# VectorE reads a chunk's second pair of value tiles out of the side bank ahead of rounding the first-layer keys' high part

## The reference, cut to what matters

```
x = x + L0_xattn(layernorm(x), ctx)     # rotary positions, a distance bias, softmax, gate
x = x + L0_ffn(layernorm(x))            # three products, tanh
x = x + L1_xattn(layernorm(x), ctx, ctx, mask)
x = x + L1_ffn(layernorm(x))            # 8 experts, the best 2 of each token

# L0_xattn, for each of 4 batches, 16 heads of 8
kv_in = layernorm(ctx, gamma, beta)
k = rope(kv_in @ Wqkv[D:2*D].T)
v = kv_in @ Wqkv[2*D:].T
attn = softmax(q @ k.T * SCALE + temporal_bias)
attended = attn @ v
```

## Time and profile before

| | |
|---|---|
| time, median of 3 runs | 558.69 us (555.54 to 559.5) |
| profiled execution, its own time | 558.84 us |
| its span, first to last instruction | 557.2 us |
| TensorE busy | 508.0 us, 91% |
| ScalarE busy | 434.7 us, 78% |
| VectorE busy | 280.2 us, 50% |
| GpSimd busy | 169.0 us, 30% |
| mean granted TensorE clock | 0.977 of 2.4 GHz |
| chain that ended last | PE 53%, ACT 12%, DVE 10%, issue 9%, POOL 8%, DMA 5% |

### The profile page before, as it was taken

How to read it: one execution, slowest core, us unless ns; L and a number is a source line. 1 busy time by engine, 2 the same in 40 slices (tenths; PEclk the granted TensorE clock), 3 DMA queues, 4 the chain that set the end, 5 groups by cost and what they waited for, 6 DMA issues and landing times.

```text
span 557.2 us, 15361 instructions
## 1 busy us (share of the span) xinstructions
PE 508.0 (91%) x6338; PEld 260.7 (47%) x6338; DVE 280.2 (50%) x739; ACT 434.7 (78%) x496; POOL 169.0 (30%) x202
## 2 busy tenths in 40 slices
PE   7788998999899898998999999899899989998995
PEld 4444545445445454554555444344443444443343
DVE  5858566874776356653522342336243533440354
ACT  1257486787678787888998999899989998999832
POOL 4468637584785308840110001000000000000000
PEclk9789899999899999999999999999999999999996
DMA  8579885389558314580745291249123910000000
GB/s 269 160 230 288 225 273 138 129 283 292 148 192 285 124 49 126 197 261 17 140 105 188 69 211 40 87 113 223 33 65 76 235 32 8 6 1 2 6 6 16
DMA packets 51584, 74.53 MB, mean 134 GB/s; under 512 B 11146, under 2 KB 40050, under 8 KB 51506
## 3 DMA queue, kind: packets, MB, share of 16 engines
q1 hardware_dynamic: 40258, 37.54, 26.9%
q0 software_dynamic: 5632, 24.07, 12.9%
q10 hardware_dynamic: 5616, 11.86, 7.0%
HBM read 39.95 MB, written 18.83 MB: 106 GB/s over the span
## 4 chain that ended last, share of the span: by engine, by line
PE 53%; ACT 12%; DVE 10%; issue 9%; POOL 8%; DMA 5%; ACTq 1%; SPq 1%; DVEq 0%; POOLq 0%
PE ps L539 24%; PE ps L515 16%; ACT probs L1171 7%; DVE k_swapped L1480 2%; DMA q_side<-in_far_q 2%; PE ps L669 2%; ACT ctx_turned L1171 2%; PE ps L440 2%; DMA ctx_tokens<-in_ctx_rows 2%; DVE row_stats L1442 1%; POOL k L1025 1%; PE ps L450 1%; ACT ctx_tokens L1171 1%; DVE k_parts L1497 1%; POOL k L1023 1%
## 5 line engine op out<-in xcount | busy, mean ns | idle before, releaser
L1171 ACT ACTIVATE probs<-ps 124x1024 f32<-124x1024 f32 (+1 forms) x305 | 295.7, 1024 | 54.2 <-PE ps L520 41.1
L515 PE MATMUL ps<-q_side,k_side 64*124 64x256 bf16 (+1 forms) x1664 | 159.9, 291 | 20.9 <-ACT probs L1171 12.1
L539 PE MATMUL ps<-probs,values 124*9 124x256 f32 (+1 forms) x2440 | 163.7, 383 | 0.0
L515 PEld LDWEIGHTS ps<-q_side,k_side 64*124 64x124 bf16 (+1 forms) x1664 | 80.0, 131 | 124.7 <-ACT probs L1171 62.0
L539 PEld LDWEIGHTS ps<-probs,values 124*9 124x9 f32 (+1 forms) x2440 | 52.9, 90 | 65.6 <-issue 15.5
L1054 POOL TENSOR_TENSOR post_rstd<-post_rstd,power 128x2 f32<-128x2 f32 x12 | 8.5, 712 | 194.0 <-DVE post_rstd L1695 126.5
L520 PE MATMUL ps<-bias_near,bias_w 64*124 64x84 bf16 (+1 forms) x416 | 42.5, 200 | 0.0
L1171 ACT ACTIVATE ctx_tokens<-ps 124x1024 f32<-124x1024 f32 (+1 forms) x37 | 37.9, 1026 | 4.9 <-PE ps L515 4.0
L1480 DVE SCALAR_TENSOR_TENSOR k_swapped<-ps,beta_products,k_table_sb 32x496 f32<-32x496 f32 (+2 forms) x64 | 40.4, 632 | 0.9
L1171 ACT ACTIVATE ctx_turned<-ps 124x1024 f32<-124x1024 f32 (+1 forms) x37 | 37.9, 1024 | 3.4 <-PE ps L515 2.4
L1171 ACT ACTIVATE ctx_normed<-ps 124x1024 f32<-124x1024 f32 (+1 forms) x37 | 37.9, 1025 | 2.4 <-PE ps L515 1.6
(11 more groups left out here) (256 smaller groups left out, 621.0 us busy)
## 6 DMA issues: line engine op xcount, KB each, us to landing
k_side<-k_scratch SPq DMA_DIRECT2D x24, 400.2 KB, 7.8
k_scratch<-k_parts POOLq DMA_DIRECT2D x16, 372.0 KB, 5.4
k_side<-k_parts SPq DMA_DIRECT2D x45, 124.0 KB, 2.5
q_side<-q_parts SPq DMA_DIRECT2D x63, 64.0 KB, 2.7
v_scratch<-values POOLq DMA_DIRECT2D x4, 936.0 KB, 10.9
values<-v_scratch SPq DMA_DIRECT2D x4, 936.0 KB, 14.4
v_scratch<-v POOLq DMA_DIRECT2D x12, 288.0 KB, 5.8
mask_q<-in_mask POOLq DMA_DIRECT2D x8, 400.5 KB, 4.4
```

Source lines behind the costliest of these rows:

```text
L515: last = pe.matmul(ps[0:width, bank, SQ * i:SQ * (i + 1)], kst[rows, j % 2, 2 * g + i, at], qst[rows, query_slot(j, run), 2 * g + i, :], s ...
L539: last = pe.matmul(ps[32 * i:32 * i + VC, ACC + g // 2, SQ * (g % 2):SQ * (g % 2) + SQ], v[0:rows, j % 2, t, h, :], probs_of(u)[0:rows, SQ ...
L1171: act.activation(probs_of(u)[0:rows, :], ps[0:rows, s:s + 2, :].rearrange("p a n -> p (a n)"), ACT.Exp)\
```

## The change

Inside `rest_of_keys`, VectorE's part after `rotate_keys`, the second pair of values is now read ahead of `high_part` in place of behind it. The number of instructions, their operands and every semaphore stay; the other four engines' programs are the same.

```diff
             def rest_of_keys(b, n):
-                both_values(b, n, 0)
+                for k in range(KEY_STEPS[n] - 1):
+                    both_values(b, n, k)
                 high_part(b, n)
-                if KEY_STEPS[n] > 2:
-                    both_values(b, n, 1)
                 middle_part(b, n)
```

## The result

The changed kernel takes **563.44 us** (median of 20 executions, 560.97 to 572.27) against 559.32 us (20 executions, 555.54 to 562.34) for the kernel before, run beside it: a ratio of 1.0075 with a 95% interval of 1.0053 to 1.0097, so 3.0 to 5.4 us slower. The forecast was 563.1 us, with a range from 557.7 to 565.2 us.

A forecast was written before the change was run, and what follows sets the result against it. The prediction took the relay of GpSimd and VectorE, not TensorE's waits, to set batch 2's end. Its terms 0.55 + 2.4 + 1.3 gave +4.3 us on 558.84, so 563.1 us, range 557.7 to 565.2.

The forecast's parts named there:

- What bounds the kernel: Batch 2: the relay between GpSimd and VectorE sets the end; TensorE's waits there, of 5.0 us over all batches, are a by-product.
- (2,1), 0: Chunk (2,1): LOW is released 1.68 us earlier, but this becomes a longer wait at the next fill of LOW; 0.
- (1,2), +0.55: Chunk (1,2): L1491 starts 0.55 us later behind the pair and the relay slips as a whole; +0.55 us.
- (2,2) and (2,3), +2.4: Batch 2: L1491 of (2,3) slips 2.48 us with a clock fall behind the fill; +2.4, or 0.9 without it.
- Nearly twice the wait that brought the clock down: At (2,2)'s fill of LOW TensorE waits 3.6 us, against 1.95 before the earlier fall, so the clock falls again.
- (3,1), 0: Chunk (3,1): TensorE gains about 1.15 us of its 1.40 but keeps it only until the exponential at 227.49; 0.
- (3,3), +1.3: Chunk (3,3): L1491 starts 2.0 us later, the sample maxima follow, and TensorE's second sample fill waits; +1.3 us.
- From 262 us on, nothing: From 262 us to the end no engine's order or release changes; the shift is only carried along.
- removed waits count: Rival: TensorE gets up to 5.0 us back, 553.8 us, or 557.7 with (3,2)'s alone; 0.18 together with no effect.
- it does nothing: Rival: the pair is no later than L1491 in any chunk, 558.8 us; inside the 0.18 shared with removed waits.
- the clock holds: Rival: same mechanism without the clock's fall in batch 2, +2.75 us, 561.6 us; chance 0.22.
- second stretch at 1.2 GHz: Rival: at (2,2)'s fill of LOW the clock stays low for two stretches, 1.6 us more, 564.7 us; chance 0.15.

The follow-up runs named there:

- early_only: Kernel before with the new order only in chunks (1,1), (2,1), (3,1) and (3,2), whose second pair was not late: 559.82 us, ratio 1.0015.
- after: The changed kernel itself, new order in all chunks, against the kernel before: 563.44 us, ratio 1.0075.
- after_again: The changed kernel run once more, word for word, against the kernel before: ratio 1.0119, few executions.
- b2_only: Kernel before with the new order in batch 2 alone: 560.3 us, ratio 1.0038.
- after_filler: The changed kernel plus 14 matmuls of zeros in TensorE's wait ahead of the fill of LOW in (2,2): ratio 1.0086 to the kernel before.
- b1_only: Kernel before with the new order in batch 1 alone: 560.22 us, ratio 1.004.
- b3_only: Kernel before with the new order in batch 3 alone: 559.23 us, ratio 1.0008.
- rows_early: Kernel before, pair in the old order, with batch 3's row statistics and GpSimd's power of them moved ahead, out of batch 2's relay: ratio 0.9999.
- late_only: Kernel before with the new order only in chunks (1,2), (2,2), (2,3) and (3,3), whose second pair was late: 562.03 us, ratio 1.0068.
- rows_early_again: The same kernel as rows_early, run again because a stall sat in the first profile: ratio 0.9991 to the kernel before.

## Why the prediction was right, and where it was off

- **What bounds the kernel.** Right. The waits of the earlier trace rows were effect, not cause; early_only took away 1.95 and 1.40 us of them without delaying the rounding anywhere and gained nothing.
- **(2,1), 0.** Right in itself: L440 no longer waits, and the time stands again as 3.49 us in front of LOW's fill (3.6 forecast).
- **(1,2), +0.55.** The slip was 0.45 us. The term was mis-sized all the same: this edit joins two waits into one of 1.43 us in front of the exponential, and in three of six traces the clock fell behind it and batch 1 cost 2.06 us. The prediction weighed the clock at one place only. A term of about half a fall's 1.6 us, +0.8, was missing here (an estimate from those traces: 2.06 less 0.46).
- **(2,2) and (2,3), +2.4.** Measured 2.33, 1.88 and 2.12 us by 210 us. The relay's part was mis-sized: L1491 of (2,3) slips by 1.9 us in after and after_again and by 2.27 in b2_only, in place of 2.48, and with the filler, without a fall, by 0.65 in place of 0.9. So the fall, forecast at 1.5 to 1.58, is worth 1.25 us in the relay (1.26 in the exponentials at 174 us). What lifts the 1.79 us at 174 to 2.33 at 210 comes in at the query DMA, whose column moves by -0.36 to +0.88 us over the runs; how much of it belongs to the edit stays open. The page "TensorE: Matmul & The Clock Gate" of the Trainium skill, section on HAM oscillation, counts half of the throttled time, and the prediction got 1.5 us from the two stretches of the earlier trace rows. The fall of the kernel before went on into the next stretch:

```profile
152.00:154.00 2.00, 2.00 (x30) 1.23 (x28) 1.95 (x16) 1.50 (x2) 1.70 (x3) 0.92 0.99 306
```

With the share of 0.08 that is missing there, the same rule gives 1.7 us, an estimate; the measured 1.26 us is below that and below the 1.58 us of the earlier trace rows.
- **"Nearly twice the wait that brought the clock down".** The conclusion held in four of four traces. The premise was weaker than it looked: waits of 1.92 to 1.99 us brought no fall in b1_only, b3_only and rows_early. One trace of before showed one outcome of two.
- **(3,1), 0.** Right. Its L440 waits 0.27 us in place of 1.40, and TensorE's L515 at 229.84 waits 0.93 us for its exponential in place of 0.38, and the next one 0.44 us.
- **(3,3), +1.3.** Right: 1.21 to 1.27 us in all six traces with the new order there. L1491 starts at 240.30; its old place, 235.15, with batch 3's shift of 3.27 us added would be 238.42, so it slips by 1.9 us (2.0 forecast), and the second sample fill waits 1.22 us.
- **From 262 us on, nothing.** Right for the edit; the last stage of a single execution moves by 2.6 us through its clock, which is why a span is a poor yardstick here.
- **The sum, +4.3.** The timed +4.1 us (3.0 to 5.4) agrees; the terms that the traces support are about 1.2 (0.45, or 2.06 in half of them), 2.1 and 1.2, in all 4.5. That the total came within 0.3 us is in part luck: 0.7 us too little in batch 1 and 0.3 us too much in batch 2 partly cancel. The rivals: "removed waits count" is out by early_only, "it does nothing" by the slips of L1491 in every trace with the new order in a late chunk; "the clock holds" is what after_filler shows, and it occurred in none of the four with the wait unfilled; no second stretch at 1.2 GHz followed the fill in (2,2), but an extra one came in batch 1, which the prediction didn't have.

## What to carry to other kernels

A wait at a buffer's release is worth something only if the next thing that its engine waits for is early; look there before moving the release, and count what the moved reads delay. Here the relay of GpSimd and VectorE decided, and in batch 2 the same reordering turned from +2.1 us to a gain of 0.5 to 1.9 us once 5 us of other work had been taken out of that relay and it was 3 us shorter per chunk. In (1,2) the same move made it dearer, because the relay then ran ahead of TensorE's fill. So compare, chunk by chunk and in the very kernel that is to be changed, when the buffer is filled with when the relay's next input comes. Small waits that are joined into one longer wait can cost more than their sum, if the clock falls behind it, as it did in three of six traces here.

## What the runs showed of the hardware

The clock doesn't follow the length of one wait alone. Behind the wait of 1.4 us for the exponential near 119 us it fell in three of six traces, but behind the wait of 1.4 us at (3,2)'s L440 in none of the seven traces that have it. Behind 1.9 to 2.0 us it fell in the kernel before, late_only and rows_early_again but not in b1_only, b3_only and rows_early, of which the last is the same kernel as rows_early_again; behind 3.5 to 3.6 us it fell in four of four. What ran behind a fall took about twice as long: the fill of 1.13 us took 1.86 to 2.04 us when it lay wholly or nearly so in the low stretch. One DMA of the distance queries, the same bytes from the same place in the program, took 9.28, 10.63 and 11.86 us from its issue to the end of the wait for it in three traces (after_filler, before, after), and so decided how much of a gain near 174 us was left at 186 us.
